# One set of four PSUM banks for the maxima and all other short uses, with row maxima of two heads read by one VectorE instruction, in a two-layer transformer kernel

## The reference, cut to what matters

```python
att = jnp.einsum('bhqd,bhkd->bhqk', q, k) * scale
att = jnp.where(causal[None, None], att, -jnp.inf)     # self-attention only
y = jnp.einsum('bhqk,bhkd->bhqd', jax.nn.softmax(att, axis=-1), v)
```

## Time and profile before

| | |
|---|---|
| median of 3 runs | 1911.96 us (1908.54 to 1912.90) |
| the profiled execution | 1909.82 us |
| its span, first to last instruction | 1908.0 us |
| mean granted TensorE clock | 0.948 of 2.4 GHz |
| busy, TensorE matmul | 1685.2 us, 88% |
| busy, VectorE | 1365.1 us, 72% |
| busy, ScalarE | 1157.9 us, 61% |
| busy, GpSimd | 657.6 us, 34% |

### The profile page before, as it was taken

One profiled execution on the slowest core, in us unless ns is written; L12 is line 12 of the kernel. 1 busy time (PEld: TensorE's weight loads), 2 busy tenths in 40 slices (PEclk: granted clock), 3 DMA queues, 4 the chain that ended last, 5 costly groups with the idle time before them and its releaser, 6 DMA issues.

```text
span 1908.0 us, 29140 instructions
## 1 busy us (share of the span) xinstructions
PE 1685.2 (88%) x10051; PEld 733.1 (38%) x10064; DVE 1365.1 (72%) x2549; ACT 1157.9 (61%) x2178; POOL 657.6 (34%) x915
## 2 busy tenths in 40 slices
PE   4898889998999989998999899998998997888677
PEld 1344334423543334323543344323443443332236
DVE  6767657777587777777687767777477687777276
ACT  1374475566755676566655585566655854856497
POOL 3432523550444224541454134532462232310040
PEclk7898889999999999999999999999998998999898
DMA  7334313322232323332242323332332232123123
GB/s 196 91 110 122 89 35 91 89 68 78 60 112 76 89 57 95 84 102 60 60 109 62 90 59 101 84 98 65 87 99 59 51 90 53 43 73 105 52 88 111
DMA packets 106947, 159.49 MB, mean 84 GB/s; under 512 B 20656, under 2 KB 83248, under 8 KB 106800
## 3 DMA queue, kind: packets, MB, share of 16 engines
q1 hardware_dynamic: 101904, 156.43, 29.6%
q10 hardware_dynamic: 4896, 1.18, 0.3%
HBM read 105.00 MB, written 51.38 MB: 82 GB/s over the span
## 4 chain that ended last, share of the span: by engine, by line
PE 55%; DVE 25%; ACT 9%; POOL 5%; issue 4%; DMA 1%; ACTq 0%; SPq 0%; DVEq 0%; POOLq 0%
DVE nmax L1267 13%; PE acc L1504 13%; PE mx L1469 11%; PE st L1490 10%; PE misc L1444 6%; PE misc L1416 4%; PE misc L1531 3%; PE misc L1456 3%; ACT probs L1000 2%; ACT tail_h L1070 2%; DVE hid L1216 2%; PE misc L1558 1%; ACT tail_h L1055 1%; ACT hid L1035 1%; POOL parts L885 1%
## 5 line engine op out<-in xcount | busy, mean ns | idle before, releaser
L1267 DVE TENSOR_REDUCE nmax<-mx 128x1 f32<-128x512 f32 (+2 forms) x1376 | 874.2, 673 | 351.2 <-PE mx L1469 209.7
L1000 ACT ACTIVATE probs<-st 128x512 f32<-128x512 f32 (+3 forms) x1536 | 766.1, 549 | 440.0 <-PE st L1490 295.7
L1469 PE MATMUL mx<-stack 96*128 96x512 bf16 (+3 forms) x1536 | 548.3, 370 | 124.9 <-DVE nmax L1267 104.3
L1490 PE MATMUL st<-stack 99*128 99x512 bf16 (+3 forms) x1536 | 546.9, 368 | 23.0 <-ACT probs L1000 21.5
L1469 PEld LDWEIGHTS mx<-stack 96*128 96x128 bf16 x1536 | 152.3, 99 | 351.2 <-DVE nmax L1267 276.5
L1490 PEld LDWEIGHTS st<-stack 99*128 99x128 bf16 x1536 | 149.5, 99 | 353.2 <-ACT probs L1000 184.6
L1504 PE MATMUL acc<-probs,v_x 128*32 128x512 f32 x1152 | 167.8, 657 | 0.0
L879 POOL TENSOR_TENSOR parts<-qk,zero 128x512 bf16<-128x512 f32 x78 | 81.2, 1041 | 216.1 <-ACT qk L983 216.1
L891 POOL TENSOR_TENSOR nparts<-nmax,zero 128x16 bf16<-128x16 f32 x96 | 21.1, 220 | 294.3 <-DVE nmax L1267 294.3
L1504 PE MATMUL acc<-probs,v_s 128*32 128x512 f32 (+3 forms) x1152 | 114.5, 470 | 0.1
L1493 PE MATMUL st<-mask_st,identb 128*128 128x128 bf16 x512 | 111.7, 221 | 0.0
(11 more groups left out here) (263 smaller groups left out, 2091.0 us busy)
## 6 DMA issues: line engine op xcount, KB each, us to landing
parts_xk<-parts SPq DMA_DIRECT2D x54, 128.0 KB
parts_xq<-parts SPq DMA_DIRECT2D x54, 128.0 KB
stack<-parts_xq SPq DMA_DIRECT2D x36, 192.0 KB, 3.2
stack<-parts_xk SPq DMA_DIRECT2D x36, 192.0 KB, 3.6
parts_sk<-parts SPq DMA_DIRECT2D x48, 128.0 KB
parts_sq<-parts SPq DMA_DIRECT2D x48, 128.0 KB
stack<-parts_sq SPq DMA_DIRECT2D x32, 192.0 KB, 2.9
stack<-parts_sk SPq DMA_DIRECT2D x32, 192.0 KB, 3.4
```

The costliest lines, as they stand in the source:

```text
L1000: act.activation(probs[:, j % P_SLOTS, c, T - w:], st_bank(n, 4 * j + c)[:, 0:w], ACT.Exp, scale=SCALE).then_inc(exp_done, 1)
L1267: dve.tensor_reduce(nmax[:, ring, first:first + NT * (len(cs) - 1) + 1:NT], src, AX.X, ALU.max, negate=True).then_inc(mx_free, 1)
L1469: last = pe.matmul(o, stack[0:ROWS, r, 0, c, P * i:P * i + P], stack[0:ROWS, r, 1, c, 0:w], start=True, stop=not causal)
L1490: last = pe.matmul(o[:, 0:w], stack[0:AUG, r, 1, c, P * j:P * j + P], stack[0:AUG, r, 0, c, T - w:T], start=True, stop=not causal)
```

## The change

The two sets of two banks become one set `misc` of four. A maxima step of one head per bank becomes a step of two heads in two neighbouring banks, with one matmul per bank as before and one VectorE reduction over both (a 128x2x512 or 128x2x384 access). `MX_FULL` falls from 16 steps to 8 and `MX_CAUSAL` from 11 to 7 (three with one bank stay). Which banks a use takes is worked out ahead by `misc_places`: a pair takes the two neighbouring banks of which the later used one was used longest ago, every other use the bank used longest ago. A PSUM use waits for the reading of the use that its bank had before; the reading is counted per bank, a pair's under its first. `BURST` becomes 4 (steps of two). The bank names in the end phase follow.

```diff
@@ -52,7 +52,7 @@
 MASKED = -3.0e38
 
 STACKS = 4
-ST_BANKS, MX_BANKS, MISC_BANKS, P_SLOTS, QK_RING = 3, 2, 2, 2, 4
+ST_BANKS, MISC_BANKS, P_SLOTS, QK_RING = 3, 4, 2, 4
...
@@ -78,9 +78,9 @@
 
-MX_FULL = [(i, [c], T) for c in range(HU) for i in range(NT)]
-MX_CAUSAL = [(0, [0, 1, 2, 3], P)] + [(1, [c, c + 1], 2 * P) for c in (0, 2)] + \
-    [(i, [c], (i + 1) * P) for i in (2, 3) for c in range(HU)]
+MX_FULL = [(i, [c, c + 1], T, 2) for c in (0, 2) for i in range(NT)]
+MX_CAUSAL = [(0, [0, 1, 2, 3], P, 1)] + [(1, [c, c + 1], 2 * P, 1) for c in (0, 2)] + \
+    [(i, [c, c + 1], (i + 1) * P, 2) for i in (2, 3) for c in (0, 2)]
 
 def exists(u, last):
...
@@ -146,7 +146,7 @@
     return out
 
-BURST = 8
+BURST = 4
 
 def slots(units, others, last, first=False):
...
@@ -180,7 +180,7 @@
 
     second = [("maxima", us[1], k) for k in banks_of(us[1])]
     return [("stack", u) for u in us[:3]] + [("maxima", us[0], k) for k in banks_of(us[0])] + [("negmax", us[0])] + \
-        second[:9] + [("negmax_T", us[0])] + second[9:]
+        second[:5] + [("negmax_T", us[0])] + second[5:]
 
 def tokens0(b):
...
@@ -301,36 +301,52 @@
 
 RING_USES = {
-    "misc": {"weights": 1, "w_row": 1, "w_tot": 1, "ctx_T": 1, "norm_T": 2, "project": 1, "v": 2, "negmax_T": 1, "heads_out": 1,
+    "misc": {"maxima": 1, "weights": 1, "w_row": 1, "w_tot": 1, "ctx_T": 1, "norm_T": 2, "project": 1, "v": 2, "negmax_T": 1, "heads_out": 1,
              "y_T": 2, "residual": 2, "quant_T": 2, "hidden": 1, "down_T": 1, "down": 1},
     "parts": {"project": 1},
 }
 
+def ring_uses(s, r):
+
+    return banks_in(s[1])[s[2]][3] if (r, s[0]) == ("misc", "maxima") else RING_USES[r].get(s[0], 0)
+
+
 def ring_starts():
     start, n = {}, {r: 0 for r in RING_USES}
-    for t, steps in enumerate(TURNS):
+    for steps in TURNS:
         for s in steps:
             start[s] = dict(n)
-            for r, uses in RING_USES.items():
-                n[r] += uses.get(s[0], 0)
+            for r in RING_USES:
+                n[r] += ring_uses(s, r)
     return start
 
 START = ring_starts()
 
-def shifted(s):
-
-    later = (s[1][0] + 1,) + s[1][1:] if isinstance(s[1], tuple) else s[1] + 1
-    return (s[0], later) + s[2:]
-
-
-RING_PER_TURN = {r: START[TURNS[2][0]][r] - START[TURNS[1][0]][r] for r in RING_USES}
-
-MX_BEFORE = [0]
-for u in ORDER:
-    MX_BEFORE.append(MX_BEFORE[-1] + len(banks_in(u)))
+def misc_places():
+
+    banks, reads, earlier = [], [], []
+    count, latest = [0] * MISC_BANKS, [-1 - MISC_BANKS + k for k in range(MISC_BANKS)]
+    for steps in TURNS:
+        for s in steps:
+            uses = ring_uses(s, "misc")
+            if s[0] == "maxima" and uses == 2:
+                first = min(range(MISC_BANKS - 1), key=lambda k: max(latest[k:k + 2]))
+                own = [(first, 1), (first + 1, 0)]
+            else:
+                own = [(k, 1) for k in sorted(range(MISC_BANKS), key=lambda k: latest[k])[:uses]]
+            for bank, reader in own:
+                earlier.append(reads[latest[bank]] if latest[bank] >= 0 else None)
+                latest[bank] = len(banks)
+                banks.append(bank)
+                count[bank] += reader
+                reads.append((bank, count[bank]) if reader else reads[-1])
+    return banks, reads, earlier
+
+
+MISC_BANK, MISC_READ, MISC_EARLIER = misc_places()
 
 class Count:
...
@@ -534,8 +543,7 @@
         w_in, w_sum, w_scale, w_quant, w_kept = \
             (sem("ffn_w_" + n) for n in ("in", "sum", "scale", "quant", "kept"))
         zeroed, waited, picked = sem("zeroed"), sem("waited"), sem("picked")
-        AHEAD = [(misc_free[0], 1), (misc_free[1], 1), (exp_done, ST_BANKS), (mx_free, MX_BANKS),
-                 (values_done, P_SLOTS), (heads_full, 1), (negmax_split, 8), (negmax_landed[0], 16),
+        AHEAD = [(exp_done, ST_BANKS), (values_done, P_SLOTS), (heads_full, 1), (negmax_split, 8), (negmax_landed[0], 16),
                  (negmax_landed[1], 16),
                  (y_summed, 1), (stored, 32)] + [(p, 48) for p in parts_out] + [(q, 4) for q in qk_split]
         VD = P_SLOTS
...
@@ -585,36 +593,34 @@
                 return dram_[b]
             return dram_[bass.ds(b, 1)].rearrange("o p t c -> p (o t) c")
 
-        def free_value(s, k=0, key=None):
-
-            return s.ring("misc", key).round(MISC_BANKS, k).at(1)
+        def misc_use(s, k=0, key=None):
+            return s.ring("misc", key).at(k)
 
         def misc_slot(s, k=0, key=None):
-            return s.ring("misc", key).slot(MISC_BANKS, k)
+            return MISC_BANK[misc_use(s, k, key)]
+
+        def misc_read(s, k=0, key=None):
+
+            return MISC_READ[misc_use(s, k, key)]
+
+        def wait_misc_read(eng, s, k=0, key=None):
+
+
+            slot, n = misc_read(s, k, key)
+            eng.wait_ge(misc_free[slot], n)
+
+        def wait_misc(eng, s, k, reads):
+
+
+            latest = {}
+            for slot, count in [x for x in [*reads, MISC_EARLIER[misc_use(s, k)]] if x]:
+                latest[slot] = max(count, latest.get(slot, 0))
+            for slot, count in latest.items():
+                eng.wait_ge(misc_free[slot], count)
 
         def wait_misc_free(eng, s, k=0):
 
-            eng.wait_ge(misc_free[misc_slot(s, k)], free_value(s, k))
-
-        def wait_misc_read(eng, s, k=0, key=None):
-
-
-            eng.wait_ge(misc_free[misc_slot(s, k, key)], s.ring("misc", key).round(MISC_BANKS, k).at(2))
-
-        def misc_read(s, k=0, key=None):
-
-            return misc_slot(s, k, key), s.ring("misc", key).round(MISC_BANKS, k).times(1, 2)
-
-        def wait_misc(eng, s, k, reads):
-
-
-            free = s.ring("misc").round(MISC_BANKS, k).times(1, 1)
-            latest = {misc_slot(s, k): free}
-            for slot, n in reads:
-                if slot not in latest or n.base > latest[slot].base:
-                    latest[slot] = n
-            for slot, n in latest.items():
-                eng.wait_ge(misc_free[slot], n.at())
+            wait_misc(eng, s, k, ())
 
         def wait_misc_full(eng, s, k=0):
...
@@ -644,8 +650,8 @@
         tail_hq = staged.rearrange("p (r f t) -> p r f t", r=2, f=KF)
         g_parts = W["Co"][:, 0, 0:C // 2].bitcast(BF16)
         turn_banks = [st[2], acc]
-        up_pairs = [st_all[:, 0:2, :], mx_all[:, :, :], misc_all[:, :, :]]
-        out_pairs = [mx, st]
+        up_pairs = [st_all[:, 0:2, :], misc_all[:, 0:2, :], misc_all[:, 2:4, :]]
+        out_pairs = [misc[0:2], st]
         t_w, t_load, t_res = sem("t_w"), [sem(f"t_load{n}") for n in range(B)], [sem(f"t_res{n}") for n in range(B)]
         t_tot, t_sc, t_full, t_gelu = sem("t_tot"), sem("t_sc"), sem("t_full"), sem("t_gelu")
         t_scaled_d, t_scaled_p, t_ints_d, t_ints_p = (sem("t_" + n) for n in ("scaled_d", "scaled_p", "ints_d", "ints_p"))
...
@@ -887,7 +893,7 @@
             def negmax(s):
                 r, done, w = s.n.slot(2), s.n.times(4, 8), HU * NT
                 part = [nparts[:, r, w * a:w * a + w] for a in range(PARTS)]
-                pool.wait_ge(mx_free, s.mx(1).at(MX_BANKS))
+                wait_misc_read(pool, s, 0, ("maxima", s.unit, banks_of(s.unit)[-1]))
                 pool.tensor_tensor(part[0], nmax[:, r, :], zero[:, :].to_broadcast([P, w]), ALU.add).then_inc(negmax_split, 1)
                 pool.wait_ge(negmax_split, done.at(1))
                 pool.tensor_tensor(nmax[:, r, :], nmax[:, r, :], part[0], ALU.subtract).then_inc(negmax_split, 1)
...
@@ -1257,15 +1263,18 @@
 
             def maxima(s):
 
-                k, n, ring = s.args[0], s.mx(), s.n.slot(2)
-                i, cs, w = banks_in(s.unit)[k]
+                k, slot, ring = s.args[0], misc_slot(s), s.n.slot(2)
+                i, cs, w, nb = banks_in(s.unit)[k]
                 if k == 0:
                     dve.wait_ge(negmax_split, s.n.times(4, 4).at())
-                dve.wait_ge(mx_full, n.at(k + 1))
-                src = mx[n.slot(MX_BANKS, k)][:, 0:len(cs) * w].rearrange("p (c k) -> p c k", k=w)
+                wait_misc_full(dve, s, nb - 1)
+                if nb == 1:
+                    src = misc[slot][:, 0:len(cs) * w].rearrange("p (c k) -> p c k", k=w)
+                else:
+                    src = misc_all[:, slot:slot + 2, 0:w]
                 first = cs[0] * NT + i
                 dve.tensor_reduce(nmax[:, ring, first:first + NT * (len(cs) - 1) + 1:NT], src, AX.X, ALU.max,
-                                  negate=True).then_inc(mx_free, 1)
+                                  negate=True).then_inc(misc_free[slot], 1)
 
             def heads_out(s):
...
@@ -1458,19 +1467,21 @@
                     last.then_inc(misc_full, 1)
 
             def maxima(s):
-                k, n, r = s.args[0], s.mx(), s.n.slot(STACKS)
-                i, cs, w = banks_in(s.unit)[k]
+                k, n, r = s.args[0], s.n, s.n.slot(STACKS)
+                i, cs, w, nb = banks_in(s.unit)[k]
                 causal = s.unit[1] == "s"
                 if k == 0:
```

(45 more changed lines are left out.)

## The result

The changed kernel takes 1888.22 us in the median of 4 runs (1887.40 to 1897.44), the kernel before 1912.43 us (4 runs). The ratio is 0.9888, with a 95% interval of 0.9854 to 0.9922. The forecast was 1889 us.

The account below looks back on a forecast made before the run. No engine is full; handovers between engines that each walk one order bound the kernel. Terms of -13 and -10 us on 1909.8 us give 1887; the median runs 2.1 us above that execution, so 1889 us, range 1875 to 1904.

Parts of the forecast that it names:

- Part 1: VectorE's maxima: fewer, longer reductions, one per pair, save 13 us (ends 0 and 28 us).
- the doubt about a read over two banks: On VectorE, a pair's read priced at 1217 ns might take 1.40 us, as ScalarE's two-bank reads suggested, undoing the saving.
- Parts 2 and 3: TensorE's waits for maxima banks: whole-pair handover and shared banks together gain 10 us; ends a 50 us gain and a loss.
- Part 2: Pair handed over whole between TensorE and VectorE: later start and release, but in a quiet place TensorE has no wait.
- Rival B: Slower: VectorE idles while a pair without a second in reserve is refilled; +22 us, 1934 us; chance 0.31.
- the loop of 1.97 us: Refill and read of a serial pair between TensorE and VectorE: 1.97 us per pair, where two queued singles take 1.19.
- Rival C: Nothing: TensorE and ScalarE pace the rest, or a two-bank read costs 1.40 us; 1908 to 1915 us; chance 0.12.
- Rival A: More is won: TensorE's long waits for maxima go too; middle some 45 us, 1867 us; chance 0.13.
- the forecast's own sign: TensorE's wait for the maxima reduction would be near 90 us, in fewer and longer waits.
- The signs: Profile checks: pair at 1.20 to 1.23 us, VectorE busy near 1267 us; wrong if TensorE's nmax waits exceed 130 us.

Follow-up runs that it names:

- e1: Changed kernel with each pair read by two reductions instead of one, both started after both matmuls and released together: 1911.4 us, 0.9994 of the kernel before.
- e3: Kernel before plus only the four shared banks; maxima stay singles in their old order: 1840.2 us, 0.9624 of the kernel before.
- e2: Changed kernel with two reductions per pair, each bank started and released by itself: 1863.5 us, 0.9739 of the kernel before.
- e8: Two kernels, e3 with one kind of use kept to two banks: only maxima may use all four, 1915.7 us; only the other uses may, 1905.6 us.
- e4: Kernel before with pairs and one reduction over both banks, maxima and other uses each keeping their own two banks: 2078.4 us, 1.0872 of the kernel before.
- e7: Changed kernel, each pair's reduction leaving out the last 128 columns of each bank: 1848.8 us, 0.9670 of the kernel before.

## Why the prediction was right or wrong

The number, the sign and the range were right, and that the number came within 1 us is luck. The sum behind it was not right: it had two small gains, and there are one large gain and two losses that nearly cancel it. In us, from the ratios times 1912:

| step | predicted | measured |
|---|---|---|
| one instruction per pair | -13 | -20 (e1 to after) |
| banks shared | part of -10 | -72 (before to e3) |
| two maxima in a row, in neighbouring banks | not priced | +22 (e3 to e2) |
| pair handed over whole | part of -10 | +49 (e2 to e1) |
| sum | -23 | -21 (medians: -24) |

- **Part 1** had the right sign, and its size lies within its ends (0 to 28 us). A pair is 1221 ns; the doubt about a read over two banks is gone. The 13 us were mis-sized: measured are 20 us, with the intervals 13 to 27. The full 28 us, which queued pairs too would win by what the prediction quotes from the Trainium skill ("VectorE: DVE Perf Modes", section "The DRAIN you can't avoid"), lies just above that. The same section of the Trainium skill goes on to say that a next operation which is not held starts earlier, and in these traces it does: two queued pairs lie 1.13 us apart under a duration of 1.22 us. One figure of this part was wrong by the prediction's own 0.09 us of overlap: VectorE's busy time was to fall by 98 us, and fell by 50 (39 from e1 to after), because busy time counts the overlap of queued reductions once and the sum of durations counts it twice. 640 pairs at 0.06 us of distance would have given 41.
- **Parts 2 and 3** are the step that failed, in the sentence "I put parts 2 and 3 together at a gain of 10 us". Together with the order they are what e1 has over the kernel before, and that is nothing (0.9994). They were weighed as half the pairs against the other half. What one pool is worth against two rings was not priced: of the misc uses only "their own ring was rarely short" was said. For the misc uses alone that was right (e8: 5 us). But the pool as a whole is worth 72 us. Part 2 counted the hand-over of a pair as a gain ("no wait"), and it costs 49 us. The gain of 10 us too many and the 7 us too few of part 1 nearly cancel, which made the number.
- **The order** was missing. Moving every second maxima step one place later, next to its neighbour, was treated as no edit at all. It costs 44 us on private banks, and with the placing in neighbouring banks 22 us on the four shared ones.
- **Rival B** had the right mechanism, and the loop of 1.97 us appears in e4. In the changed kernel its cost (49 us) is real and is covered by the sharing. The sign of B's case was avoided by a term that the prediction had not seen.
- **Rival C** fell: TensorE and ScalarE do not hide VectorE's time entirely, a quarter shows (e7). **Rival A** fell too: the waits of TensorE for nmax stayed near 92 us, as the forecast's own sign said (near 90), in fewer and longer waits (115 of 0.80 us on average, where there were 164 of 0.64).
- **The signs** did not warn. The last one, VectorE's idle time ahead of nmax growing by more than its busy time falls, came near: it grew by 38 us against 50. None of the signs could tell a sum of small terms from one of large ones.
- **Slips.** The window from 1160 to 1180 us is the fullest of those with maxima, but not of all (1840 to 1860 us has 18.60 us of VectorE). In rival B, 0.2 us per serial pair and 0.07 us can't both be the price from which it decides; by its own product, 326 x 0.07 = 23, it is 0.07.

Why the pool is worth so much is argued from the e8 runs and the one stretch shown; how the 72 us spread over the stages was not measured.

## What to carry to other kernels

Buffers that several kinds of work use in turn can be worth more as one pool, each use taking the one used longest ago, than as rings of their own, even if no ring seems short; in this kernel four banks gave 3.8% and seven 5.1%. A rule that makes uses take neighbours narrows the pool again: count how far back each use reaches. Joining two reads into one instruction saves its fixed cost, but count what it gives up: the consumer starts later, the first buffer comes back later, and the producer's steps bunch up. When a change has several parts, a right total proves none of them: run each part alone, since here the best version was the change without the part that it was named after.

## What the runs showed of the hardware that was not expected

A VectorE reduction over two PSUM banks costs no more for the second bank than its columns: 1221 ns for 2 x 512 columns and 956 ns for 2 x 384, within 5 ns of the slope of the single banks (685 and 552 ns). ScalarE's 1.20 us for two banks in the earlier trace rows did not carry over to it. Queued reductions overlap also at this size: two pairs in a row span 2.35 us (timeline of VectorE in the changed kernel), 1.13 us from start to start under a duration of 1.22.

```profile
611.01 2.35 DVE L1276 TENSOR_REDUCE nmax<-misc 128x2 f32<-128x1024 f32 x2
```
